# One-hot batches in longer runs, two halves of a weight tensor waited for apart, one cast moved to ScalarE

## The reference

```python
h = jnp.maximum(_layernorm(x, axis=-1), 0.0)
# layer 0, on h
h = jax.nn.sigmoid(x @ wenc.T + benc)            # encoder, 1024 -> 500
h2 = h @ conv_weight                             # the convolution's product
msgs = h2[src] * edge_weight[:, None]            # 20000 edges, sorted by dst
agg = jax.ops.segment_sum(msgs, dst, num_segments=x.shape[0])
hout = agg + h @ lin_weight.T
p = hout @ wdec.T + bdec
# layer 1, on the result: h = x @ W.T + b, then a sum over edges and self loops,
# scaled by deg[row]**-0.5 * deg[col]**-0.5
```

## Time and profile before

| | |
|---|---|
| median of three runs | 463.01 us (462.94 to 463.04) |
| the profiled execution | 463.1 us, span of the core 461.1 us |
| TensorE busy (matmuls) | 455.7 us, 99% of the span |
| VectorE | 294.8 us, 64% |
| ScalarE | 210.2 us, 46% |
| GpSimd | 170.3 us, 37% |
| granted TensorE clock | 1.000 of full speed |

### The profile page before, as it was taken

How to read it: one execution, slowest core, us unless ns; L and a number is a source line. 1 busy time by engine, 2 the same in 40 slices (tenths; PEclk the granted TensorE clock), 3 DMA queues, 4 the chain that set the end, 5 groups by cost and what they waited for, 6 DMA issues and landing times.

```text
span 461.1 us, 7281 instructions
## 1 busy us (share of the span) xinstructions
PE 455.7 (99%) x3128; PEld 364.5 (79%) x2628; DVE 294.8 (64%) x504; ACT 210.2 (46%) x389; POOL 170.3 (37%) x159
## 2 busy tenths in 40 slices
PE   8999999999999999999999999999999999999997
PEld 6999999988888889888878774444459888777776
DVE  6989778799767198136099797795311194444443
ACT  6898885854576214214334566332325612221210
POOL 1500000000030027291269888200004699896550
PEclk9999999999999999999999999999999999999999
DMA  8620005000000136200199900553320233613113
GB/s 321 257 92 2 1 2 179 1 2 1 1 1 2 57 121 235 100 0 1 56 407 155 167 1 1 199 234 131 133 114 1 79 130 150 224 42 90 45 44 94
DMA packets 26317, 44.70 MB, mean 97 GB/s; under 512 B 15526, under 2 KB 15837, under 8 KB 25639
## 3 DMA queue, kind: packets, MB, share of 16 engines
q1 hardware_dynamic: 26024, 43.77, 29.6%
q0 software_dynamic: 224, 0.39, 0.3%
q10 hardware_dynamic: 30, 0.02, 0.0%
HBM read 27.53 MB, written 13.41 MB: 89 GB/s over the span
## 4 chain that ended last, share of the span: by engine, by line
PE 94%; DVE 3%; ACT 1%; DMA 1%; POOL 1%; issue 0%; DVEq 0%
PE ps L1668 90%; PE ps L1672 2%; PE ps L1686 2%; DMA xn<-in_x_dram 1%; POOL wehi L684 1%; DVE xn L1291 0%; DVE m_hot L1226 0%; DVE s_hot L1223 0%; DVE stats L1132 0%; ACT C L888 0%; DVE stats L1133 0%; DVE cvlo L1238 0%; ACT A_all L889 0%; ACT cvhi L953 0%; DVE m_hot L1221 0%
## 5 line engine op out<-in xcount | busy, mean ns | idle before, releaser
L1668 PE MATMUL ps<-CT,ghi 125*128 125x500 f16 (+1 forms) x240 | 77.0, 339 | 0.0
L1668 PE MATMUL ps<-CT,glo 125*128 125x500 f16 (+1 forms) x240 | 76.9, 339 | 0.0
L796 POOL TENSOR_TENSOR S<-U_all 128x500 f32<-128x500 f32 x25 | 31.7, 1280 | 77.7 <-DVE Blo L1625 58.5
L1651 DVE SCALAR_TENSOR_TENSOR x1b<-ps,dsc,x1b 125x512 f32<-125x512 f32 x49 | 35.2, 746 | 35.0 <-PE ps L1668 34.6
L704 POOL TENSOR_TENSOR C<-C,loops 125x125 f16<-125x125 f16 x10 | 3.7, 413 | 110.0 <-DVE got L1410 110.0
L1668 PE MATMUL ps<-A_lo,h2hi 125*125 125x500 f32 (+1 forms) x120 | 42.3, 353 | 0.0
L1668 PE MATMUL ps<-Bhi,Shi 128*125 128x512 f32 (+1 forms) x144 | 39.4, 388 | 0.0
L1668 PE MATMUL ps<-Blo,Shi 128*125 128x512 f32 (+1 forms) x144 | 39.3, 388 | 0.0
L1668 PE MATMUL ps<-zhi,wehi 128*125 128x250 f32 x160 | 39.1, 287 | 0.2 <-POOL wehi L684 0.2
L1668 PEld LDWEIGHTS ps<-CT,ghi 125*128 125x128 f16 x240 | 23.5, 98 | 19.1 <-issue 0.3
L1668 PEld LDWEIGHTS ps<-CT,glo 125*128 125x128 f16 x240 | 23.4, 98 | 18.8
(11 more groups left out here) (196 smaller groups left out, 1138.9 us busy)
## 6 DMA issues: line engine op xcount, KB each, us to landing
xn<-in_x_dram SPq DMA_DIRECT2D x10, 512.0 KB, 6.1
x<-in_x_dram SPq DMA_DIRECT2D x10, 512.0 KB
x_scratch<-x SPq DMA_DIRECT2D x10, 500.0 KB
x1b<-x_scratch SPq DMA_DIRECT2D x10, 500.0 KB
out_dram<-x1b SPq DMA_DIRECT2D x19, 240.0 KB
B<-in_W_dram SPq DMA_DIRECT2D x4, 1024.0 KB, 8.5
c_scratch<-C SPq DMA_DIRECT2D x10, 305.2 KB
wd<-in_wdec_dram SPq DMA_DIRECT2D x1, 2048.0 KB, 15.6
```

The source lines that it names most:

```text
L796: p.tensor_tensor(S32[m][:, :, :], quarter(u, *one_of), quarter(u, *other), op).then_inc(*S_ok.up(u, m))
L1651: v.scalar_tensor_tensor(r, ps[bank8["w", u, m]][0:PB, 0:512], scale, r, ALU.mult, ALU.add).then_inc(*term_ok.up(u, m, n))
L1668: return t.matmul(o_ap, lhsT, rhs, start=start, stop=stop)
```

## The change

Three edits. First, `adjs` is rewritten for slots 10 to 15: slots 10, 12 and 14 read no batch, slot 11 reads batches 0 and 1, slot 13 batches 2 and 3, slot 15 batches 4 and 5. ScalarE's copies follow `adjs`; VectorE's building (`hots`) stays. Second, the second half of f=1 of `wehi` is cast by ScalarE behind the four `z_hi` of the first blocks instead of by GpSimd as the last of three. Third, VectorE's `conv_lo(0)` moves from the end of slot 17 (ahead of that slot's `enc_lo`) to the start of slot 18, and slot 20 waits for each half of `cvhi` and `cvlo` where it first reads it.

```diff
     adjs = [[]] + hots[:-1]
+    for s in (11, 13, 15):
+        adjs[s - 1:s + 1] = [[], adjs[s - 1] + adjs[s]]
...
-    whi_p = signal("whi_p", [(0, 1), (1, 0), (1, 1)])
-    whi_a = signal("whi_a", [(0, 0), (2, 0), (3, 0)])
+    whi_p = signal("whi_p", [(0, 1), (1, 0)])
+    whi_a = signal("whi_a", [(0, 0), (1, 1), (2, 0), (3, 0)])
...
-        return whi_p.at(f, h) if (f, h) in whi_p.values else whi_a.at(f, 0)
+        return whi_p.at(f, h) if (f, h) in whi_p.values else whi_a.at(f, h if f < 2 else 0)
...
-        def wenc_hi(f, k1=KB):
+        def wenc_hi(f, k0=0, k1=KB):
             a.wait_ge(*d_we[f].at())
-            a.activation(wehi[f][:, 0:k1, :], we32[f][:, 0:k1, :], ACT.Copy).then_inc(*whi_a.up(f, 0))
+            a.activation(wehi[f][:, k0:k1, :], we32[f][:, k0:k1, :], ACT.Copy).then_inc(*whi_a.up(f, k0 // 4))
...
-        wenc_hi(0, 4)
+        wenc_hi(0, 0, 4)
         for k, h in FIRST:
             z_hi(k, h)
+        wenc_hi(1, 4, 8)
         block_mean(3)
...
-            if s == 19:
-                conv_lo(1)
+            if s in (18, 19):
+                conv_lo(s - 18)
             for i in hots[s][:1]:
                 hot_batch(i)
...
-            if s == 17:
-                conv_lo(0)
             if slot[0] == "enc":
                 enc_lo(s)
...
-            if k == 0:
-                t.wait_ge(*cvhi_ok.at(1))
             for j in range(FB):
+                if k == 0 and j % 2 == 0:
+                    t.wait_ge(*cvhi_ok.at(j // 2))
...
                 mm(o_ap, H, cvhi[0:PB, j, :], j == 0, False)
-                if (k, j) == (0, 0):
-                    t.wait_ge(*cvlo_ok.at(1))
+                if k == 0 and j % 2 == 0:
+                    t.wait_ge(*cvlo_ok.at(j // 2))
```

## The result

| | before | after |
|---|---|---|
| median of 16 runs each | 462.98 us (462.77 to 463.32) | 463.82 us (463.68 to 464.15) |
| ratio after to before | | 1.0018, 95% interval 1.0011 to 1.0026 |
| the profiled execution | 463.1 us, span 461.1 | 463.68 us, span 461.9 |
| span, mean of the runs | 461.01 to 461.06 us (groups below) | 462.01 us |

The change makes the kernel 0.84 us slower. The forecast was 464.3 us, +1.27 in its own sum, with a range of 463.3 to 464.8: the sign and, in the main, the mechanism held, the sum was half as large again as what was measured.

The account below looks back on a forecast made before the run. TensorE was taken to bound the kernel nearly from start to end, unbroken from 128.19 us on. Terms +1.75 - 0.33 - 0.15 = +1.27 us on the profiled 463.1 gave 464.4, forecast as a 464.3 us median, range 463.3 to 464.8.

Parts of the forecast that it names:

- the forecast's own case: Sum of all terms, 464.3 us, own range 464.0 to 464.6, chance 0.50.
- the rival with 464.0: GpSimd's third cast slows VectorE's first welo, so its removal starts slot 11 0.30 us earlier; chance 0.15.
- The start: TensorE's 0.36 us wait at 14.32 for GpSimd's cast goes, but is lost again at block 7; worth 0.
- The third cast and `welo`: welo stands behind GpSimd's second cast, so removing the third gives VectorE 0; welo stays at 1.49 us.
- Batch 0: Moved behind slot 11, its windows leave a hole before block 7's transposes (still 50.24); slot 12 starts 0.97 us later.
- Batch 2, T: Moved behind slot 13, it saves one return to the encoder, -0.08 us; slot 13's windows start at T = 61.72.
- Block 9's wait: Transposes wait for z_lo of block 8; slot 13's windows to slot 15 take 7.32 us, 0.86 behind no wait.
- The rival without this wait: ScalarE has unseen slack in slot 13, so block 9's transposes do not wait: 463.4 us, chance 0.12.
- Banks: Four units on three banks: 0.11 us of room, 0 taken; rival of 0.1 to 0.2 in two runs, 464.6, chance 0.13.
- Sum of the first edit: Slot 16 starts 0.78 + 0.97 = 1.75 us later than before.
- The convolution: Batches 10 and 11 ready earlier, -0.33 us; the 0.30 wait for cvlo at 90.37 goes, taken as -0.15.
- The faster rival: Blocks 7 and 9's transposes wait only for TensorE's own windows, z_lo of block 6 by 48.7: 461.7 us, chance 0.10.

Follow-up runs that it names:

- late_gather: Kernel before, with GpSimd's four gathers waiting for the second normalization: 463.13 us, ratio 1.0001.
- cast_two: Kernel before with both halves of f=1 of wehi cast by ScalarE, GpSimd keeping one cast: 463.07 us, ratio 1.0004.
- pairs_only: Kernel before with the first edit alone (batches 0 to 5 read in three runs of two): 464.90 us, ratio 1.0039.
- The early order: z_hi of blocks 6 and 8 ahead of z_relu of 7 and 9, their z_lo ahead of the batch; on the changed kernel 461.73 us.
- early_nopairs: Changed kernel without its first edit, z_hi of blocks 6, 8 ahead of z_relu of 7, 9, their z_lo ahead of the batch: 461.61 us.
- cast_late: Kernel before with the second edit, and GpSimd's four gathers waiting for the second normalization: 462.83 us, ratio 0.9996.
- conv_only: Kernel before with the third edit alone (conv_lo of half 0 behind enc_lo, halves waited for apart): 462.47 us, ratio 0.9987.
- cast_only: Kernel before with the second edit alone (one cast from GpSimd to ScalarE): 462.70 us, ratio 0.9992.

## Why the prediction was right, and where its sum was off

The measured 463.82 lies in the range, but below the 464.0 to 464.6 that the forecast's own case was given, and 0.12 below the 463.94 above which the prediction had put 0.71 of its chances. It is nearer to the rival with 464.0 than to the forecast.

- **The start.** TensorE's wait for GpSimd goes and its 0.36 us is lost again in front of block 7: right. That the rest of the machine gets nothing earlier was wrong. The step that failed is "neither ScalarE nor VectorE gets it earlier": it counted what the moved cast does to ScalarE and to `welo`, but not that the gathers queued behind it on GpSimd start 1.5 us sooner. That spares `ry` 0.18 us, and `ry` heads the chain to block 7. Nor did it count that ScalarE's sigmoids at 22.7 would otherwise wait for TensorE: the 0.36 is no gain of TensorE's own, but without it VectorE's 0.18 is held up there, as late_gather shows. Term taken 0, measured -0.38: 0.20 of it in the mean span and 0.18 outside it, where the prediction took the time as given.
- **The third cast and `welo`.** Right: 1.49 stays, and it is 1.20 in cast_two, where the second cast is gone. The Trainium skill (SBUF — State Buffer, Who interferes with whom) says that a GpSimd instruction that reads SBUF and a VectorE operation with two inputs in SBUF take turns for whole instructions, and that the 0.29 (1.49 less 1.20) vanishes with the cast agrees with that in kind. In size it agrees less well: a `welo` that began only when the cast ended at 12.75 would come 0.45 later, not 0.29. The rival with 464.0 named the wrong mechanism, although VectorE's gain, which it put at 0.30, was there at 0.18 by way of `ry`. That its time came out nearest is luck.
- **Batch 0.** Right: the hole is 1.06 us of listed wait in pairs_only and 1.23 in after. In after's profiled execution block 7's transposes stand at 49.78, not 50.24, and 0.26 of that belongs to this execution: `x` arrived early, VectorE's first statistics begin at 4.28 instead of 4.54. The rest is the 0.18 of `ry`. That is also why the profiled execution shows 0.69 at 128 us and the runs a mean span 0.95 to 1.00 longer.
- **Batch 2, T.** Right, 61.68 for 61.72.
- **Block 9's wait.** Right in place and size, as a sum: 7.38 from T to slot 15 in after and in pairs_only (69.06), for 7.32 forecast; against the 6.46 without a wait that is 0.92, for 0.86. The rival without this wait is refuted.
- **Banks.** Right. No wait lies inside any run of windows, so that rival is refuted too.
- **Sum of the first edit**: 1.75 forecast, 1.82 measured.
- **The convolution.** Right in kind, 0.13 short in size. The batch's 0.33 is exact. The wait for `cvlo` of 0.30 was counted by half, because a late load hides in part behind the matmul in front; the runs give 0.28, nearly all of it.
- **The faster rival.** Its condition, `z_lo` of block 6 by 48.7, was not met in after. The early order meets it by 47.4, and early_nopairs, though without the pairs, came to 461.61, where that rival had 461.7.

The sum with measured terms is 1.82 - 0.61 - 0.38 = +0.83 for +1.27 forecast: +0.07, -0.13 and -0.38 by term. The first edit is the whole of the loss, and it loses because it takes windows away from the two places where TensorE, without them, waits for `z_lo`.

## What to carry to other kernels

Filler work of the critical engine is worth its place more than its switching cost: a saved return is 0.08 us, a filler taken from in front of a wait cost 0.97 at block 7 and, together with ScalarE's four units, 0.92 at block 9. Before work is bundled, ask of each place where it stood what the engine would wait for without it, and make that ready earlier first: here the three bundles then cost 0.12 us instead of 1.82, and the reordering alone brought 0.50. When an instruction leaves a queue, all that is queued behind it moves up, and what it then stands beside has to be read as well. And a gain of one engine lasts only to the next point where it meets one that gained nothing: late_gather and cast_two both sped VectorE up, and lost the gain again behind a TensorE that was late.

## What the runs showed of the hardware

- **A gather on GpSimd and small VectorE work.** A two-column integer operation takes 0.17 us, and 0.34 or 0.35 when it starts 0.62 or 0.63 us into the second `sdw` gather; 0.11 to 0.14 us into the second `ww` gather it takes 0.17, and 0.17 without a gather beside it (late_gather, cast_late). Before, pairs_only and conv_only show the long time, the ten kernels with a cast moved and late_gather the short one.
- **A gather behind a two-input VectorE operation.** A gather alone takes 0.99 to 1.00 us. In cast_only the first starts at 12.94 and takes 1.88, to 14.82, while `welo` runs to 13.78: it ends 1.04 behind `welo`, as if it had begun there. In cast_two it takes 2.12 from 12.33 on and ends 1.03 behind a `welo` that ends at 13.42. In the kernel before, where it starts behind `welo`, it takes 1.16.

```profile
12.94 1.88 POOL L675 DMA_INDIRECT sdw<-in_sd_rows_dram,row_i  x1 [0.20 <-issue]
15.12 0.99 POOL L677 DMA_INDIRECT ww<-in_w_rows_dram,row_i  x1 [0.31 <-issue]
```

- **The time outside the span** is not a constant of the kernel: 1.81 to 1.85 us in all kernels with a cast moved and gathers as early as GpSimd can, 2.01 to 2.03 in those with neither, 2.15 with late gathers alone and 2.01 with both. Here that was 0.18 us, half of what the cast's edit brought.
- **The arrival of the first input** varies by execution: VectorE's first statistics begin between 4.28 and 4.63 us in the profiled executions, and all that hangs on the start chain shifts with it. Two profiled executions compared at 50 us carry this difference.
